# Start of a fused attention and quantised-FFN kernel: when the right-hand matrix is loaded, and where the FFN of chunks 0 and 1 and the LayerNorm of chunks 4 and 5 stand

## The reference

```python
xn = layernorm(x)                        # x: (16, 2048, 1024) f32
q, k, v = xn @ Wq.T, xn @ Wk.T, xn @ Wv.T          # 16 heads of 64
s = window_attention(q, k, v, 128) @ Wo.T          # each row sees the last 128 keys
# FFN: both sides quantised to int8, rows of xn and columns of rhs by absmax
lhs_scale = absmax(xn, axis=-1) / 127;  rhs_scale = absmax(rhs, axis=0) / 127
g = silu((round(xn / lhs_scale) @ round(rhs / rhs_scale)) * lhs_scale * rhs_scale)
y = x + s * g
```

## Time and profile before

| what | value |
|---|---|
| median of three runs | 710.84 us |
| profiled execution | 712.11 us, of which its slowest core's span is 710.5 us |
| spans of the eight cores | 703.9 to 710.5 us |
| TensorE busy in the span | 94% |
| VectorE, ScalarE, GpSimd busy | 67%, 49%, 24% |
| mean granted TensorE clock | 0.985 of full |

### The profile page before, as it was taken

One profiled execution on the slowest core, in us unless ns is written; L12 is line 12 of the kernel. 1 busy time (PEld: TensorE's weight loads), 2 busy tenths in 40 slices (PEclk: granted clock), 3 DMA queues, 4 the chain that ended last, 5 costly groups with the idle time before them and its releaser, 6 DMA issues.

```text
span 710.5 us, 17009 instructions; the slowest of 8 cores (703.9 to 710.5 us)
## 1 busy us (share of the span) xinstructions
PE 665.4 (94%) x5724; PEld 413.0 (58%) x5724; DVE 475.9 (67%) x958; ACT 346.7 (49%) x473; POOL 172.6 (24%) x281
## 2 busy tenths in 40 slices
PE   1897769989999999999999999999999999999995
PEld 0682436555666666565666666565666666556642
DVE  4644577766776677766766667766766677664485
ACT  1342665544554445554554445554554445453442
POOL 4323311322222222121222222121222222120122
PEclk9998979999999999999999999999999999999999
DMA  9999913735655454656757445545555445543234
GB/s 191 149 200 188 182 18 76 149 119 134 134 129 127 119 88 97 131 120 134 134 120 127 115 102 94 130 120 134 135 122 125 115 92 104 131 89 76 76 90 149
DMA packets 109859, 86.40 MB, mean 122 GB/s; under 512 B 92112, under 2 KB 92240, under 8 KB 109776
## 3 DMA queue, kind: packets, MB, share of 16 engines
q1 hardware_dynamic: 104880, 76.83, 47.4%
q0 software_dynamic: 4608, 8.39, 8.4%
q10 hardware_dynamic: 288, 0.10, 0.1%
HBM read 54.62 MB, written 16.78 MB: 100 GB/s over the span
## 4 chain that ended last, share of the span: by engine, by line
PE 87%; DVE 5%; DMA 4%; issue 2%; POOL 1%; ACT 1%; DVEq 0%; SPq 0%; ACTq 0%; POOLq 0%
PE pj L675 44%; PE pj L666 29%; PE psc L759 5%; PE pav L783 4%; PE pav L785 2%; DMA xs<-x 2%; DMA wv<-wvt 2%; DVE ee L356 1%; PE pav L666 1%; PE psc L666 1%; DVE sm L326 1%; DVE gg L385 0%; DVE sm L291 0%; DVE sm L403 0%; POOL aot L831 0%
## 5 line engine op out<-in xcount | busy, mean ns | idle before, releaser
L573 ACT ACTIVATE ee<-psc 128x1024 bf16<-128x1024 f32 (+1 forms) x128 | 128.4, 1003 | 157.8 <-PE psc L759 152.9
L825 POOL TENSOR_TENSOR xr<-tt,xr 128x512 f32<-128x512 f32 x63 | 80.4, 1277 | 370.0 <-DVE tt L391 344.6
L675 PE MATMUL pj<-wv,xnt 128*128 128x512 bf16 x480 | 118.7, 391 | 5.1 <-DMA wv<-wvt 3.8
L675 PE MATMUL pj<-qrhs,qlt 128*128 128x512 bf16 x512 | 122.0, 382 | 0.0
L675 PE MATMUL pj<-wo,aot 128*128 128x512 bf16 x512 | 116.4, 379 | 1.2 <-ACT aot L313 1.2
L666 PE MATMUL pj<-xnt,wq 128*128 128x256 bf16 x960 | 112.3, 276 | 1.9 <-DVE xnt L311 1.8
L666 PE MATMUL pj<-xnt,wk 128*128 128x256 bf16 x960 | 109.7, 273 | 0.0
L356 DVE TENSOR_TENSOR ee<-ee,mask_s 128x1024 bf16<-128x1024 bf16 (+1 forms) x128 | 104.1, 813 | 7.6 <-ACT ee L573 2.1
L666 PEld LDWEIGHTS pj<-xnt,wq 128*128 128x128 bf16 x960 | 93.1, 99 | 13.5 <-issue 2.1
L666 PEld LDWEIGHTS pj<-xnt,wk 128*128 128x128 bf16 x960 | 92.0, 98 | 10.3
L675 PEld LDWEIGHTS pj<-wo,aot 128*128 128x128 bf16 x512 | 49.5, 98 | 60.0 <-issue 1.7
(11 more groups left out here) (122 smaller groups left out, 661.5 us busy)
## 6 DMA issues: line engine op xcount, KB each, us to landing
xs<-x SPq DMA_DIRECT2D x32, 512.0 KB, 6.7
xr<-x SPq DMA_DIRECT2D x32, 512.0 KB, 7.2
y<-xr SPq DMA_DIRECT2D x31, 512.0 KB, 8.2
wq<-wqt POOLq DMA_DIRECT2D x8, 256.0 KB, 10.4
wk<-wkt POOLq DMA_DIRECT2D x8, 256.0 KB, 11.1
wv<-wvt POOLq DMA_DIRECT2D x8, 256.0 KB, 8.3
wo<-wot POOLq DMA_DIRECT2D x8, 256.0 KB, 10.1
xr<-rhst SPq DMA_DIRECT2D x3, 512.0 KB, 5.8
```

The lines of the kernel that those rows point to most:

```text
L573: op(lambda: a.activation(o, i, AF.Exp, scale=0.125), "a", ("exp", c, b))
L675: yield [lambda kc=kc: t.matmul(p[:], src[:, off + kc * step:off + kc * step + 128], w[:, kc * 1024 + j * 512:kc * 1024 + (j + 1) * 512], ...
L825: op(lambda: p.tensor_tensor(r, tt[h], r, ALU.add), "p", ("add", c, h))
```

## The change

The left and right FFN halves of chunks 0 and 1, with all of TR and both RS, stand between K and V. All eight pieces of rhs have a buffer (the eighth is the exp buffers `ee`, now one tensor) and are loaded at once when piece 5 of Wk has landed; pieces of Wv are issued in pairs between the casts on GpSimd; pieces 6 and 7 are scaled on GpSimd (`rq_p`) and not on ScalarE. LN, quantisation and transposition of chunks 4 and 5 stand beside V. Chunks 0 and 1 keep only V of 4 and 5 in their gaps. x of chunks 1 and 3 is issued from ScalarE, and Wq waits for x of chunk 0. Q of pair 0 does six of its steps before TX of 2 and 3. At the end the last transposition of `ao` stands between the two O halves.

```diff
 def slot_gaps(c):
-    if c == 0:
-        return [halves("TX", 4, 5), halves("V", 4)[:1], halves("V", 4)[1:], []]
-    if c == 1:
-        v, f1 = halves("V", 5), [("F", i, 1) for i in range(2)]
-        return [halves("TR", 4, 5), v[:1] + halves("TR", 6, 7), v[1:] + [("RS", 0, 1)] + f1[:1], f1[1:]]
+    if c < 2:
+        v = halves("V", c + 4)
+        return [v[:1], [], v[1:], []]
 def pe_order():
-    out = one(halves("TX", 0, 1)) + [("G", q0, range(4))] + one(halves("TX", 2)) + [("G", q0, range(4, 5))]
-    out += one(halves("TX", 3)) + [("G", q1, range(5)), ("G", q0, range(5, 6)), ("G", q1, range(5, 6))]
+    out = one(halves("TX", 0, 1)) + [("G", q0, range(6))] + one(halves("TX", 2, 3)) + [("G", q1, range(6))]
     out += one(halves("TL", 0, 1))
+    for h in range(2):
+        out += one(halves("TR", *range(4 * h, 4 * h + 4)) + [("RS", 0, h), ("F", 0, h), ("F", 1, h)])
+    out += one(halves("TL", 2, 3))
     out += [("G", v0, range(4)), ("G", v1, range(4))] + each(v0 + v1, range(4, 8))
-    out += one(halves("TL", 2, 3) + halves("TR", 0, 1, 2, 3) + [("RS", 0, 0), ("F", 0, 0), ("F", 1, 0)])
+    out += one(halves("TX", 4, 5))
...
-    out += [("G", [g], range(6)) for g in last] + one([("TA", NC - 1, 3)])
+    out += [("G", last[:1], range(6))] + one([("TA", NC - 1, 3)]) + [("G", last[1:], range(6))]
 def evacuator(g):
+    if k in ("TX", "TR") and i >= 4:
+        return "a"
 def emit_sync(sync):
-            for c in range(4):
+            load_x(sync, 0)
+            load_x(sync, 2)
+            landed(sync, "wk5", 0)
+            for i in range(8):
+                load_rh(sync, i)
+            for c in range(4, 7):
                 load_x(sync, c)
-            landed(sync, "wk4", 0)
-            for i in range(4):
-                load_rh(sync, i)
-            landed(sync, "wv2", 0)
-            load_x(sync, 4)
-            load_x(sync, 5)
-            landed(sync, "wv6", 0)
-            for i in range(4, 8):
-                load_rh(sync, i)
-            load_x(sync, 6)
+            t_ql(sync, 4)
+            t_ql(sync, 5)
 def emit_vector(v):
...
-            evac_v(v, ("K", 1, 0))
-            evac_v(v, ("K", 1, 1))
+            for g in range(4):
+                evac_v(v, ("K", 1, g))
             rabs(v, 2)
-            evac_v(v, ("K", 1, 2))
-            evac_v(v, ("K", 1, 3))
             evac_v(v, ("TL", 0, 0))
             evac_v(v, ("TL", 1, 0))
-            ql(v, 2)
-            ql(v, 3)
             rabs(v, 3)
             rscale(v, 2)
             rdiag(v, 0)
+            evac_v(v, ("TR", 0, 0))
+            evac_v(v, ("TR", 1, 0))
+            rabs(v, 4)
+            evac_v(v, ("TR", 2, 0))
+            rabs(v, 5)
+            rscale(v, 4)
+            evac_v(v, ("TR", 3, 0))
+            rabs(v, 6)
+            zev(v, 0, 0)
+            rabs(v, 7)
+            rscale(v, 6)
+            gate(v, 0, 0)
+            zev(v, 1, 0)
+            rdiag(v, 1)
+            gate(v, 1, 0)
+            ql(v, 2)
+            ql(v, 3)
             bn(v, 4)
             bn(v, 5)
+            for c in range(2):
+                zev(v, c, 1)
+                gate(v, c, 1)
+            xn(v, 4)
+            xn(v, 5)
             evac_v(v, ("TL", 2, 0))
             evac_v(v, ("TL", 3, 0))
+            for c in (4, 5):
+                amax(v, c)
+                ql(v, c)
 def emit_scalar(a):
             op(lambda: a.dma_start(ident[:], ident_h[:]), "li", 0, 16)
+            load_x(a, 1)
+            load_x(a, 3)
...
-            for g in halves("V", 0, 1, 2, 3):
-                evac_a(a, g)
-            for g in halves("TL", 2, 3) + halves("TR", 0, 1, 2, 3) + [("RS", 0, 0)]:
-                evac_a(a, g)
-            cen(a, 4)
-            cen(a, 5)
+            for i in range(4):
+                evac_a(a, ("TR", i, 1))
+            evac_a(a, ("RS", 0, 0))
             rq(a, 4)
             th(a, 0, 0)
             rq(a, 5)
             th(a, 1, 0)
+            for g in halves("TR", 4, 5, 6, 7):
+                evac_a(a, g)
+            evac_a(a, ("RS", 0, 1))
+            th(a, 0, 1)
+            th(a, 1, 1)
+            evac_a(a, ("TL", 2, 1))
+            evac_a(a, ("TL", 3, 1))
+            cen(a, 4)
+            cen(a, 5)
+            for g in halves("V", 0, 1):
+                evac_a(a, g)
+            qp(a, 4)
+            qp(a, 5)
+            for g in halves("V", 2, 3) + halves("TX", 4, 5):
+                evac_a(a, g)
+        def rq_p(p, i):
+            need(p, "v", ("rsc", i - i % 2))
+            st = stage[i]
+            op(lambda: p.tensor_scalar(st, st, sm[:, C_RSC + i:C_RSC + i + 1], MAGIC, ALU.mult, ALU.add),
+               "p", ("rq", i))
 def emit_gpsimd(p):
-            load_w(p, 0, range(2))
-            need(p, "v", ("bn", 0))
-            load_w(p, 0, range(2, 4))
+            landed(p, "lx0", 0)
+            load_w(p, 0, range(4))
...
-            landed(p, "rh1", 0)
-            load_w(p, 2, range(4))
-            rcast(p, 0)
-            rcast(p, 1)
-            load_w(p, 2, range(4, 8))
-            rcast(p, 2)
-            rcast(p, 3)
+            for i in range(0, 6, 2):
+                rcast(p, i)
+                rcast(p, i + 1)
+                load_w(p, 2, range(i, i + 2))
+            for i in (6, 7):
+                rq_p(p, i)
+                rcast(p, i)
+            load_w(p, 2, range(6, 8))
             rstd(p, 4)
-            landed(p, "rh6", 0)
             load_w(p, 3, range(8))
-            for i in range(4, 8):
-                rcast(p, i)
```

More of the change, by code:

```diff
@@ L119, in build @@
     groups = list(dict.fromkeys(g for o in order if o[0] == "G" for g in o[1]))
-    early = halves("TX", 2, 3) + [("Q", 1, g) for g in range(4)] + [("K", 1, g) for g in range(4)]
-    early += halves("V", 2, 3) + halves("TL", 2, 3) + halves("TR", 0, 1, 2, 3) + [("RS", 0, 0)]
+    wide = halves("TX", 2, 3) + halves("V", 2, 3) + halves("TL", 2, 3) + halves("TR", *range(8))
+    wide += [(k, 1, g) for k in "QK" for g in range(4)] + [("RS", 0, 0), ("RS", 0, 1)]
+    early = [g for g in groups if g in wide]
     bank, before = {}, {}
@@ L141, in build @@
         vv = [sb(f"vv{i}", VW, BF16) for i in range(VR)]
-        ee = [sb(f"ee{i}", 1024, BF16) for i in range(4)]
+        eb = sb("ee", 4096, BF16)
+        ee = [eb[:, i * 1024:(i + 1) * 1024] for i in range(4)]
         ao = [sb(f"ao{i}", 1024, BF16) for i in range(2)]
@@ L163, in build @@
         names += [f"{n}{i}" for n in ("txn", "tql", "tao") for i in range(2)]
-        names += [f"rh{i}" for i in range(7)]
+        names += [f"rh{i}" for i in range(8)]
         S = {n: es.enter_context(nc.semaphore("s_" + n)) for n in names}
@@ L196, in view @@
             return bass.AP(t, off, [[t.shape[1], 128]] + [list(d) for d in dims])
-        stage = [gg[0], gg[1], zb, tb, xr[0], xr[1], xr[2], tb]
-        rst_bf = [aot[0], aot[1], ao[0], ao[1]] + aot * 2
+        stage = [t[:] for t in gg + [zb, tb] + xr] + [eb[:, 0:2048].bitcast(F32)]
+        rst_bf = (aot + ao) * 2
         def emptied(eng, g):
@@ L273, in emit_sync @@
                     load_xr(sync, c - 1)
-                if c >= 2:
+                if c >= 4:
                     store(sync, c - 2)
@@ L277, in emit_sync @@
                     t_xn(sync, c + 4)
-                if c < NC - 4:
+                if 2 <= c < NC - 4:
                     t_ql(sync, c + 4)
+                if c in (2, 3):
+                    store(sync, c - 2)
             load_xr(sync, NC - 1)
@@ L374, in zev @@
                 emptied(v, ("RS", 0, h))
-                need(v, "p", ("rcast", 3))
+                need(v, "p", ("rcast", 3 if h == 0 else 7))
             else:
@@ L454, in emit_vector @@
             evac_v(v, ("TX", 2, 0))
+            evac_v(v, ("TX", 3, 0))
             ql(v, 0)
             amax(v, 1)
-            evac_v(v, ("TX", 3, 0))
             ql(v, 1)
             amax(v, 2)
-            amax(v, 3)
             for g in range(4):
                 evac_v(v, ("Q", 1, g))
+            amax(v, 3)
             rabs(v, 0)
@@ L477, in emit_vector @@
             rdiag(v, 0)
+            evac_v(v, ("TR", 0, 0))
[15 more added lines that the diff above has]
+            ql(v, 3)
             bn(v, 4)
             bn(v, 5)
+            for c in range(2):
[3 more added lines that the diff above has]
+            xn(v, 5)
             evac_v(v, ("TL", 2, 0))
             evac_v(v, ("TL", 3, 0))
[L482 to L495, removed]
+            for c in (4, 5):
+                amax(v, c)
+                ql(v, c)
+            extra = {}
             held, gates = None, []
@@ L825, in add @@
             op(lambda: p.tensor_tensor(r, tt[h], r, ALU.add), "p", ("add", c, h))
+        def rq_p(p, i):
[3 more added lines that the diff above has]
+               "p", ("rq", i))
         def rcast(p, i):
-            need(p, "a", ("rq", i))
+            if i < 6:
+                need(p, "a", ("rq", i))
+            else:
+                own(p, "p")
             if i >= 4:
```

(4 more changed lines are left out.)

28 lines of the change are left out of this document (13 added, 15 removed).

## The result

The changed kernel takes **721.96 us** (median of four runs, 721.21 to 722.92), the kernel before 711.15 (median of four; the 710.84 ahead was that of three): ratio 1.0156, 95% interval 1.0136 to 1.0176. It is slower by 11 us, clear of the noise though under 2%, and 5 us above the top of the forecast range of 702 to 717. The profiled execution of the changed kernel took 721.21 us. All its cores are alike, with spans of 716.2 to 719.7 us; of before they were 703.9 to 710.5.

What follows compares the result with a forecast made beforehand. It took a full TensorE behind a prologue as the bound, so chunk 2's start sets the end: +0.4 there, -0.6 in the tail, -0.2 in sum, 710.6 against the median of 710.84, rounded to 710 us; range 702 to 717.

Steps and rivals of the forecast that it cites:

- K's end to the first F: Prologue after K: scaling, casting and transposing rhs 2 and 3 let F start at 58.5 us, 10.3 us after K.
- F to the end of rcast 7: Between the two FFN halves: scaling and casts of rhs 5 to 7 end at 71.4 us, 12.9 us after F starts.
- V to chunk 2: From V's start at T = 79.3 through chunks 0 and 1: chunk 2 starts at T+37 = 116.3 us, +0.4 against before.
- The start: TX, Q and K in the prologue: earlier x and six Q steps first bring K's end from 52.1 to 48.2 us.
- Holding Wq: At kernel start: Wq held until x of chunk 0 is there brings x2 and x3 to about 10 to 11 us.
- the loop `zev`, tanh, `rq` 5: Between the FFN halves: `rq` 5 stands behind chunk 0's tanh, which waits for `zev`, which waits for F; ends 64.6 us.
- The ends of 1.04 and 2.55: Cost of one `rq_p` on GpSimd ahead of the right FFN half: 1.1 us taken, 1.04 below, 2.55 above (+2.9 in all).
- the loop through `ql` 4 and `amax` 5: Behind V, ScalarE and VectorE wait on each other: a 4.4 us wait without counterpart before, first V half then 3.5 us.
- Rival B: Chunks 0 and 1 run cold: three other V halves take 3.5 us, +5.2, 715 to 716 (718 with dear `rq_p`); chance 0.20.
- C: Ahead of the right FFN half, rhs pieces land late behind Wv loads: another 3 us late gives 714 us; chance 0.07.
- the wait before TR 2: Sign the forecast is right: TensorE waits 4 us before transposing rhs piece 2, between K and the left FFN half.
- the wait for the V copies: Sign the forecast is right: a 4 us wait for ScalarE's V or TX copies behind TX of 5.

## Why the prediction was wrong

Each interval of the working against core 0 of the trace, in us:

```
stage                       forecast   measured   difference
to the end of K                 48.2       50.6         +2.4
K's end to the first F          10.3       11.7         +1.4
F to the end of rcast 7         12.9       14.2         +1.3
rcast 7 to V                     7.9        8.1         +0.2
V to chunk 2                    37.0       39.3         +2.3
start of chunk 2               116.3      123.9         +7.6
first Q of chunk 2 cold          0          1.7         +1.7
```

The profile says 719.7 for a forecast span of 710.3. The two totals of the table make 9.3 of the 9.4.

**The start** failed at "the `xn` of chunks 0 and 1 move from 14 to about 12". They are at 14.06. x of chunk 1 landed at 9.67 (8.22 before) and `bn` ended at 11.3, but then GpSimd's small steps of `rstd` follow, 2.4 us. First VectorE's `xn`, then the first and last of the six steps:

```profile
14.06 1.53 DVE L322 TENSOR_SCALAR xnr<-xs,sm 128x1024 bf16<-128x1024 f32 x2 [1.30 <-POOL sm L841]
```

```profile
11.51 0.19 POOL L831 TENSOR_SCALAR sm<-sm 128x2 f32<-128x2 f32 x1 [2.48 <-DVE sm L294]
...
13.75 0.20 POOL L841 TENSOR_TENSOR sm<-sm 128x2 f32<-128x2 f32 x1
```

Before, these steps ran from 10.06 to 12.50, hidden by `bn` of chunk 2, which held VectorE until 13.97; the prediction reckons with x landing sooner and has no term for the steps. So with chunk 1 landing as before `xn` could start at 12.5, not 12, and chunk 1 landed 1.45 us later. Everything up to K's end is late by the same 2.4 us: Q starts at 18.37 for 16, Q of pair 1 at 27.91 for 25.5. Holding Wq brought chunks 2 and 3 sooner, which the path did not wait for.

**K to F**: the order of the queues was right almost to the instruction. With K's end 2.4 later, `rq` 2 and 3 should end at 57.6 and `rcast` 3 at 58.7; they end at 57.65 and 58.86. The wait was 5.40 where 4 was named. What failed is, first, that TR 2 and 3 and RS were costed warm: 3.9 us from TR 2 to the end of RS, which alone takes 1.10 and not 2.02 in the run with idle matmuls. There F starts 11.0 us behind K's end and here 11.7, so the clock is 0.7 of the 1.4. The rest is VectorE's row: its copy of TR 3 ends 10.8 us behind K's end (61.44), and the working had it start at 10.2 and left out its length of 0.42.

**F to `rcast` 7**: the loop `zev`, tanh, `rq` 5 was named with its order, and the run that takes it apart gives 3.4 us back, so it was real. Up to the end of the Wv issues the working was right to 0.2 us (8.2 behind F for 8.4). The 1.3 us come behind them, most from `rq_p`: 1.13 us for the first, as taken, but 2.06 for the second, beside `ql` and `bn` on VectorE. The ends of 1.04 and 2.55 that the prediction kept did hold it.

**V to chunk 2**: the loop through `ql` 4 and `amax` 5 was named and costed at a wait of 4.4; it was 3.87 and 0.85, 4.7 in all. The loop stood late as a whole. Its first link, "ScalarE copies V of 1 at T+11", ended at T+12.4 (97.03, after waits of 0.26 and 0.62 us inside V and with the copy's own 0.59), and the first score product came at T+20.0 and not T+18.3. The slots added the other 0.6: S to chunk 2 took 19.3 for 18.7.

**The clock of chunk 2** was not in the sum. Rival B looked for cold V halves in chunks 0 and 1; one took 3.11, and the other cold stretch fell on Q, behind the thin slots that B named. This is the one term that the sum put at nothing: the first Q of chunk 2 at half clock for part of its way, +1.7. The row of before on which B rested, 100 to 105, was read as score and value products between waits; it holds the transpositions of TR 4 and 5 too, and a wait of 2.33 us for their copy. What slots with nothing but scores and values do, only after shows.

**The range.** Every interval came out late and none early, although the F pairs came shorter than costed (4.4 us for 6.5, 4.2 for 5.2). The range allowed for some of the terms to fall early; in this chain of waits none did. The rivals were priced one at a time (B at 715 to 718, C at 714), and what came was the late parts of several at once. Of the signs that the prediction named, the wait before TR 2 and the wait for the V copies were there, and the first F pair ran at a clock of 0.58, not 0.5; the waits before TR 6 and 7 were 3.1 and 2.3 with a third of 2.5 before TR 5; K's end and chunk 2 came late. So the loops and waits that the prediction named were there, and in the right order. What failed were four sizes, `xn` at 12 (+2.4), TR, RS and VectorE's row ahead of F (+1.4), the second `rq_p` (+1.3) and ScalarE's row behind V with the slots (+2.3), and one term left out, the cold Q (+1.7).

**What the change lost.** This is another question than what the forecast missed. Runs gave back 3.1 us in the loop behind V, 3.4 in the loop ahead of `rcast` 7 and 3.2 of cold clock in the F stages, together 9.7 of the 11; all three were in the forecast's sum, at about their size. Under them lies the decision to put the right half ahead of V. The kernel that leaves it in chunks 0 and 1 is 16.6 us faster than the change; it also moved the quantisation of chunk 5 and the rest of the rhs chain, so how much the place alone is worth stays open, and the 9.7 us overlap with the 16.6. The 2.4 us of `rq_p` lie in the same stage as the loop ahead of `rcast` 7, and the two were not tried together. Left open: why rhs 0 is there 4 us apart on two cores.

## What to carry to other kernels

Put a chain between engines beside bulk work that does not need it; moved in front, every hop of it is paid, and what follows the waits may run at half clock as well. When you sum a prologue, list every engine's small steps between two named events, also those that something else hides today, and let the upper end of the range hold the case that all stages in a row fall late. Idle matmuls in a wait are a cheap test of how much of a loss is the clock, provided that they stand ahead of the wait and not behind it.

## What the runs showed of the hardware

When VectorE and GpSimd worked at once on tensors in SBUF, one or the other took longer. `gate` of 512 elements took 1.96 us beside GpSimd's `rq_p` and 0.69 without, while that `rq_p` took 1.13. `ql` 2 and 3 took 2.12 for two beside GpSimd, and 1.29 in the run with only the left half ahead of V, where GpSimd only issued DMAs meanwhile:

```profile
61.63 1.29 DVE L343 TENSOR_SCALAR qlr<-xs 128x1024 bf16<-128x1024 f32 x2
```

The second `rq_p`, beside `ql` and `bn`, took 2.06. Only for `gate` did an edit take the GpSimd work away.
